# Second sorting pass carries projected rows, one stream for both directions of the first layer, and stage ends without the GpSimd drain

## The chip, the cores and the metric

The kernel runs on one core of a Trainium2 chip. The metric is the device time of one execution in microseconds (us). Its engines: PE (TensorE), DVE (VectorE), ACT (ScalarE), POOL (GpSimd) and SP (SyncE, which here only issues DMAs).

## The reference, cut to what matters

Four graph layers over N = 6250 nodes with 128 features and E = 106250 edges. Each is added to its input and normalized. The first is attention in both directions of every edge; layer 1 (two HGT sublayers), layer 2 (GCN) and layer 3 (GINE) go along `dst` alone.

```python
def _attention_aggregate(h_proj, sender, receiver, attn_vec, num_nodes):   # 4 heads of 32
    e = (h_proj[sender] . attn_vec[:, :HD]) + (h_proj[receiver] . attn_vec[:, HD:])
    e = leaky_relu(e, 0.2)
    alpha = exp(e - segment_max(e, receiver)[receiver])
    alpha = alpha / (segment_sum(alpha, receiver)[receiver] + 1e-8)
    return segment_sum(h_proj[sender] * alpha, receiver)
# layer 0: in = aggregate(src -> dst), out = aggregate(dst -> src),
#          y = layernorm(x @ W_self + in + out + bias); x = layernorm(x + y)
```

## The kernel before, in words

Nodes are padded to NB = 49 blocks of 128 (partition = node within the block). Edges lie in 128 partitions of EC = 832 columns. The program is 14 stages, one `Space` each; a stage allocates its buffers and semaphores, holds one block of five engine programs, and ends with engine drains, the clearing of its semaphores by GpSimd and a barrier of all engines (lines 59 to 70). Where the profile names L67 or L70, it means this end.

1. `load_inputs` and `count_keys` load the keys and count the edges of each node by `dst`.
2. `place_edges(k=1)` ("plc1") and `place_edges(k=0)` ("plc0") are two counting sorts, by `dst` and by `src`. Both read the input order `REC` (partner key, key, type, weight: RW = 4 words) and work in NCH = 104 chunks of CH = 8 columns. PE, DVE and ACT work out a slot for each of the 128 x 8 edges; POOL then issues 8 indirect DMAs (L843), each of which scatters 128 rows of 16 bytes into `slots`. `idx` has IB = 4 buffers, so DVE (`finish`, L637 to L645) may be at most four chunks ahead of what has landed. plc1 also counts by `src` (`count_more`) and zeroes DRAM. plc0 also projects x (`project`: PE L737 to L751, DVE `pack`), writes the row `h, scores` to `table0`, keeps x @ W_self in `g.HH` in SBUF, scatters the first-of-node scores of the `dst` side (L850), and builds the tables of the `dst` order (`table_part`).
3. `layer0_sweeps` ("l0") goes over the 832 columns twice, side 1 (`dst` order), then side 0 (`src` order): 104 chunks of CK = 16 columns. For each column POOL issues one indirect DMA (L951) that gathers 128 rows of W0 = 136 words from `table0` by the partner's number; `G` has GR = 4 chunk buffers. DVE's `logits` (L1082 to L1096) makes the scores and a running maximum; ACT (`powers`) makes the exponentials in PSUM (L1025 to L1029); DVE multiplies the rows (L1103) and scans them (L1108), the segment sum; ACT copies the result to `ROW` (L1037, L1038) and SP stores it to `sums`. DVE does these steps of one chunk before it begins the next. Beside it POOL also scatters 49 blocks of scores (L959) and fetches 49 blocks of sums of side 1 (L983), which DVE adds to `g.HH`. At the end of a side a short merge joins the partitions (L1119 to L1142, POOL L936 and L942).
4. `turn_layer` ("t0", "t1", "t2") fetches the last row of each node from `sums` by 49 indirect DMAs (L1682), normalizes groups of GT = 7 blocks on DVE and ACT (`close_part` in t0, seven parts that run seven blocks ahead), and projects block by block on PE; POOL scatters the queries of each block (L1689), from four buffers `qr`.
5. `attention_sweep` (L1245, rows of 256 words, twice), `plain_sweep` (L1501, twice), `turn_plain` and `close_all` do the other layers in the same way.

What sets the order: every engine runs its own program in order, written out by hand. POOL's queue carries all indirect DMAs; SP's carries the plain loads and stores; ACT's carries `low_rows` in the placings.

Of the kernel before, what the change touches and what calls it, by code (L numbers as in the profile page):

```python
# [5 lines left out]
P = 128  # L6
# [24 lines left out]
NCK = EC // CK  # L31
GR = 4
# [7 lines left out]
RW = 4  # L40
PART = 32
W0 = D + 2 * H
# [12 lines left out]
class Space:  # L55
# [22 lines left out]
    def sem(self, name):  # L78
        self.sems.append(self.nc.alloc_semaphore(f"{self.tag}_{name}"))
        return self.sems[-1]  # L80

    def block(self):
        return self.ctx.enter_context(self.nc.Block())
# [48 lines left out]
def load_inputs(nc, g, a):  # L132

    with Space(nc, "ld") as s:
# [34 lines left out]
        def _(pool):  # L169
# [17 lines left out]
            pool.iota(g.col[:, :], pattern=[[1, EC]], base=-EC, channel_multiplier=0,  # L187
                      allow_small_or_imprecise_dtypes=True).then_inc(made, 1)
# [8 lines left out]
        def _(v):  # L197
# [6 lines left out]
            v.wait_ge(made, 13)  # L204
# [16 lines left out]
            for k in (1, 0):  # L221
                v.tensor_copy(g.REC[:, :, k], keys[:, k, :])
# [3 lines left out]
                v.tensor_copy(g.LOW[:, k, :], lo[:, :])  # L226
                link(v.tensor_copy(g.DIG[:, k, 1, :], hi[:, :]))
            v.wait_ge(drawn_p, 2)
            v.tensor_copy(g.REC[:, :, 3], weights[:, :])
            link(v.tensor_copy(g.REC[:, :, 2], keys[:, 2, :]))  # L230
# [50 lines left out]
def count_keys(nc, g, a, k, tag):  # L281

    with Space(nc, tag) as s:
# [22 lines left out]
        def _(sp):  # L306
# [14 lines left out]
        def _(act):  # L321
            for c in range(3, NCH, 4):
                if c >= OB:
                    act.wait_ge(counted, c - OB + 1)
                for x in range(CH):
                    o = act.activation(column(olo[:, c % OB, :, :, :], x), g.iota_b[:, :], ACT.Square, scale=-1.0,
                                       bias=g.LOW[:, k, c * CH + x:c * CH + x + 1])
# [29 lines left out]
        def _(pe):  # L357
            pe.wait_ge(zeroed, 1)
            pe.matmul(pc[:, 0:NB], zero[:, :], zero[:, 0:NB], start=True, stop=False, skip_group_check=True)
            for c in range(NCH):  # L360
# [9 lines left out]
                if c in (8, 16):  # L370
                    n = c // 8 - 1
                    for q, (start, z) in enumerate(wide):
                        o = pe.transpose(px[0:z, n, q * P:(q + 1) * P], g.LOW[:, 1 - n, start:start + z], g.ident[:, :])
# [8 lines left out]
class Tables:  # L382


    def __init__(self, s):
# [6 lines left out]
        self.small = s.sb("tab_small", [P, 8])  # L392
        self.diag = s.sb("tab_diag", [P, 3, P])
        self.bc = s.sb("tab_bc", [P, 3, P])


TABLE_PARTS = 13
# [10 lines left out]
def table_part(v, link, g, b, k, pb, i):  # L408

    F, t, small, diag, bc = b.F, b.t, b.small, b.diag, b.bc  # L410
    own = b.rec[:, :, k]
    if i == 0:
        v.wait_ge(b.loaded, 32)
        v.tensor_copy(g.OTHI[:, k, :], b.rec[:, :, 1 - k])
    elif i == 1:
        if k == 1:
            v.scalar_tensor_tensor(out=g.KVI[:, :], in0=b.rec[:, :, 0], scalar=float(R), in1=b.rec[:, :, 2],
                                   op0=ALU.mult, op1=ALU.add)
            v.tensor_copy(g.WEIGHT[:, :], b.rec[:, :, 3])
    elif i == 2:  # L420
        v.tensor_tensor(F[:, 1:EC], own[:, 1:EC], own[:, 0:EC - 1], ALU.not_equal)
        link(v.tensor_tensor(F[:, 0:1], own[:, 0:1], b.prev[:, :], ALU.not_equal))
    elif i == 3:
        link(v.tensor_tensor(t[:, :], g.slot[:, :], F[:, :], ALU.mult))
        link(v.tensor_reduce(small[:, 0:1], t[:, :], AX.X, ALU.max))
    elif i == 4:
        link(v.tensor_tensor(t[:, 1:EC], g.col[:, 1:EC], F[:, 1:EC], ALU.mult))
        link(v.tensor_reduce(small[:, 1:2], t[:, 1:EC], AX.X, ALU.min))
    elif i == 5:
        v.tensor_scalar(diag[:, 0, :], g.ident[:, :], small[:, 0:1], None, ALU.mult)  # L430
        v.tensor_scalar(diag[:, 1, :], g.ident[:, :], own[:, 0:1], None, ALU.mult)
        v.tensor_scalar(diag[:, 2, :], g.ident[:, :], own[:, EC - 1:EC], None, ALU.mult).then_inc(b.ruled, 1)
    elif i == 6:
        v.wait_ge(b.spread, 1)
        v.tensor_copy(bc[:, :, :].rearrange("p a b -> p (a b)"), pb).then_inc(b.read, 1)
        v.wait_ge(b.read, 1)
        link(v.tensor_tensor(bc[:, 0, :], bc[:, 0, :], g.after[:, :], ALU.mult))
        link(v.tensor_reduce(small[:, 2:3], bc[:, 0, :], AX.X, ALU.max))
    elif i == 7:
        link(v.tensor_scalar(small[:, 2:3], small[:, 2:3], -1.0, g.head[:, 0:1], ALU.add, ALU.subtract))  # L440
        link(v.tensor_scalar(small[:, 3:4], F[:, 0:1], -1.0, 1.0, ALU.mult, ALU.add))
        link(v.tensor_tensor(small[:, 2:3], small[:, 2:3], small[:, 3:4], ALU.mult))
    elif i == 8:
        v.tensor_scalar(g.SEGI[:, k, :], small[:, 2:3], g.head[:, 0:1], None, ALU.add)
        v.tensor_copy(g.HEADI[:, k, :], g.head[:, :])
        link(v.tensor_scalar(small[:, 4:5], small[:, 1:2], float(EC - 1), g.head[:, 0:1], ALU.add, ALU.add))
        v.tensor_copy(g.FIRSTI[:, k, :], small[:, 4:5])
    elif i == 9:
        link(v.tensor_scalar(small[:, 5:6], small[:, 4:5], g.idle[:, 0:1], None, ALU.subtract))
        link(v.tensor_tensor(small[:, 5:6], small[:, 5:6], small[:, 3:4], ALU.mult))  # L450
        link(v.tensor_scalar(g.BACKI[:, k, :], small[:, 5:6], g.idle[:, 0:1], None, ALU.add))
    elif i == 10:
        link(v.tensor_scalar(bc[:, 1, :], bc[:, 1, :], own[:, EC - 1:EC], None, ALU.is_equal))
        link(v.tensor_tensor(g.MM[:, k, :], bc[:, 1, :], g.before[:, :], ALU.mult))
        link(v.tensor_scalar(bc[:, 2, :], bc[:, 2, :], own[:, 0:1], None, ALU.is_equal))
    elif i == 11:
# [2167 lines left out]
```

## Time and profile before

| what | us |
|---|---|
| three runs, median (lowest to highest) | 9965.67 (9952.68 to 9969.04) |
| the profiled execution, its own time | 9951.04 |
| its span, first to last instruction | 9949.3 |
| POOL busy | 6849.4 (69%) |
| DVE busy | 5464.7 (55%) |
| ACT busy | 3065.5 (31%) |
| PE busy | 2007.9 (20%) |
| DMA moved | 1161.90 MB, 117 GB/s |

Busy time does not count the time in which an engine's sequencer issues or waits. A row of a group of instructions has its count, its busy time, the mean of one in ns, and the idle time of the engine before them with what ended it; "issue" is time without a wait that the profile shows.

### The profile page before, as it was taken

Reading aid. Unit: us, or ns where it says so; the run is one execution under the profiler, and the core shown is the slowest. Engines: PE = TensorE matmul, PEld = TensorE weight load, DVE = VectorE, ACT = ScalarE, POOL = GpSimd, SP = SyncE. Lnnn points to the kernel's source line nnn. Section 1 sums busy time; section 2 is a strip of 40 time slices with the busy share of each in tenths; the row PEclk is TensorE's granted clock in tenths of the full one; section 3 lists DMA queues with packets and bytes.
Section 4 is the critical chain, followed back from the end, with each engine's and each line's share of the span. In section 5 each row is a group of like instructions: output and inputs, shape, how many; then the busy total and the mean of one; then the engine's idle time right before and its main releaser. Section 6 shows DMA issues by size and latency. Waiting matters only on the chain. (4 is left out here: it accounts for less than half of the span.)

```text
span 9949.3 us, 59877 instructions
## 1 busy us (share of the span) xinstructions
PE 2007.9 (20%) x16169; PEld 1858.3 (19%) x16169; DVE 5464.7 (55%) x9481; ACT 3065.5 (31%) x3237; POOL 6849.4 (69%) x7186
## 2 busy tenths in 40 slices
PE   5555465550000000002500007000032000200002
PEld 5555455550000000002500007000021000100002
DVE  7555454443545554556688884788874222432225
ACT  6333233331223332232355543454531000110002
POOL 3777677777777777775477763677745777577773
PEclk5555555555555555556855558555555555555556
DMA  5411111112333333334466654566642333233331
GB/s 163 147 28 29 33 35 34 33 29 64 99 99 115 110 110 107 104 113 138 166 217 211 213 192 168 192 214 213 212 140 77 105 103 108 82 96 104 105 107 58
DMA packets 490844, 1161.90 MB, mean 117 GB/s; under 512 B 184121, under 2 KB 279692, under 8 KB 432396
## 3 DMA queue, kind: packets, MB, share of 16 engines
q0 software_dynamic: 255936, 474.70, 17.8%
q1 hardware_dynamic: 204620, 628.82, 17.3%
q10 hardware_dynamic: 29952, 54.54, 2.0%
q8 instruction: 133, 2.18, 0.1%
q14 instruction: 203, 1.66, 0.1%
HBM read 669.61 MB, written 487.92 MB: 116 GB/s over the span
## 5 line engine op out<-in xcount | busy, mean ns | idle before, releaser
L843 POOL DMA_INDIRECT slots<-REC,plc_idx x1664 | 1597.8, 960 | 551.2 <-issue 505.6
L951 POOL DMA_INDIRECT l_G<-table,OTHI x1664 | 1585.8, 953 | 513.4 <-issue 505.6
L1245 POOL DMA_INDIRECT l_swp_G<-table,KVI x1664 | 1573.4, 946 | 529.2 <-issue 506.3
L1501 POOL DMA_INDIRECT l2s_G<-table,OTHI x832 | 785.0, 943 | 389.7 <-issue 253.3
L1501 POOL DMA_INDIRECT l3s_G<-table,OTHI x832 | 786.4, 945 | 301.6 <-issue 253.3
L714 PEld LDWEIGHTS plc_pr<-plc_seen,plc_otf 128*128 128x128 f32 x3328 | 846.6, 324 | 20.5 <-issue 11.8
L714 PE MATMUL plc_pr<-plc_seen,plc_otf 128*128 128x49 f32 x3328 | 847.7, 409 | 10.9 <-DVE plc_seen L628 10.9
L1348 DVE SCALAR_TENSOR_TENSOR l_swp_QS<-l_swp_QS,KEEP,l_swp_QX 128x128 f32<-128x128 f32 x1664 | 589.1, 354 | 45.6 <-DMA l_swp_QX<-queries 8.3
L645 DVE TENSOR_SCALAR plc_idx<-plc_pos 128x8 uint32<-128x8 f32 x208 | 36.4, 175 | 946.0 <-DMA slots<-REC,plc_idx 945.3
L1103 DVE TENSOR_TENSOR l_X<-l_G,l_AW 128x2048 f32<-128x2048 f32 x104 | 397.3, 3821 | 217.7 <-ACT l_X L1029 210.8
L1108 DVE TENSOR_TENSOR_SCAN l_X<-l_AW,l_X 128x2244 f32<-128x2244 f32 x104 | 502.5, 4832 | 3.6
L1407 DVE TENSOR_TENSOR_SCAN l_swp_X<-l_swp_AW,l_swp_X 128x2244 f32<-128x2244 f32 x104 | 501.5, 4822 | 0.1
L1082 DVE TENSOR_TENSOR l_LB<-l_RE,l_G 128x64 f32<-128x64 f32 x104 | 29.6, 284 | 793.7 <-DMA l_G<-table,OTHI 793.5
L1457 PE MATMUL l_swp_AW<-l_swp_ET,ones 128*128 128x512 f32 x4 | 4.2, 1142 | 2169.4 <-DVE l_swp_ET L1437 2169.4
L716 PEld LDWEIGHTS plc_pr<-plc_ohi,plc_bm 128*128 128x128 bf16 x1664 | 440.6, 265 | 0.0
L1296 ACT ACTIVATE l_swp_VT<-l_swp_G 128x2048 f32<-128x2048 f32 x104 | 385.9, 3711 | 73.7 <-DMA l_swp_G<-table,KVI 66.5
L1313 ACT ACTIVATE l_swp_ROW<-l_swp_X 128x2112 f32<-128x2112 f32 x104 | 407.6, 3919 | 0.0
L1038 ACT ACTIVATE l_ROW<-l_X 128x2112 f32<-128x2112 f32 x104 | 407.4, 3917 | 0.0
L1457 PEld LDWEIGHTS l_swp_AW<-l_swp_ET,ones 128*128 128x128 f32 x4 | 1.0, 312 | 2169.8 <-DVE l_swp_ET L1437 2169.8
L1578 DVE SCALAR_TENSOR_TENSOR l2s_S<-l2s_ROW,KEEP,l2s_G 128x128 f32<-128x128 f32 x52 | 18.7, 360 | 704.1 <-DMA l2s_G<-table,OTHI 704.1
L1578 DVE SCALAR_TENSOR_TENSOR l3s_S<-l3s_ROW,KEEP,l3s_G 128x128 f32<-128x128 f32 x52 | 18.7, 360 | 701.6 <-DMA l3s_G<-table,OTHI 701.6
L1186 PE MATMUL l_pr<-l_ET,ones 128*128 128x512 f32 x4 | 4.1, 1126 | 1958.8 <-DVE l_ET L1122 1958.8
(488 smaller groups left out, 9261.4 us busy)
## 6 DMA issues: line engine op xcount, KB each, us to landing
sums<-l_ROW SPq DMA_DIRECT2D x104, 1088.0 KB, 4.2
sums<-l_swp_ROW SPq DMA_DIRECT2D x104, 1088.0 KB, 5.2
l_swp_QX<-queries SPq DMA_DIRECT2D x104, 1024.0 KB, 8.0
queries<-plc_zrow SPq DMA_DIRECT2D x33, 1664.0 KB
sums<-l3s_ROW SPq DMA_DIRECT2D x52, 1032.0 KB, 4.3
plc_low<-low_rows ACTq DMA_DIRECT2D x208, 256.0 KB
sums<-l2s_ROW SPq DMA_DIRECT2D x52, 1024.0 KB, 4.4
table<-t_row SPq DMA_DIRECT2D x98, 512.0 KB, 2.9
```

The source lines that it names most:

```text
L714: pe.matmul(pr[:, b, j * NB:(j + 1) * NB], otf[:, c % FB, j, :], seen[:, b, :, j], start=True, stop=False)
L716: last = pe.matmul(pr[:, b, j * NB:(j + 1) * NB], bm[:, b, j, :], column(ohi[:, c % HB, :, :, :], j), start=False, stop=True)
L843: pool.indirect_dma_start(out=slots, out_offset=bass.IndirectOffsetOnAxis(ap=idx[:, c % IB, j:j + 1], axis=0), in_=g.REC[:, c * CH + j, :] ...
L951: pool.indirect_dma_start(out=G[:, c % GR, j, :], out_offset=None, in_=table, in_offset=bass.IndirectOffsetOnAxis(ap=g.OTHI[:, side(c), x: ...
L1038: act.activation(ROW[:, c % 2, :, 0:D + H], X[:, c % 2, :, :, 1:CK + 1].rearrange("p h d c -> p c (h d)"), ACT.Copy).then_inc(rowed, 1)
L1103: v.tensor_tensor(X[:, b, :, 0:HD, 1:CK + 1], G[:, c % GR, :, 0:D].rearrange("p c (h d) -> p h d c", h=H), W[:, :, :].rearrange("p h (o c) ...
L1108: v.tensor_tensor_scan(X[:, b, :, :, :].rearrange("p h d c -> p (h d c)"), AF[:, :, :, :].rearrange("p h d c -> p (h d c)"), X[:, b, :, :, ...
L1245: pool.indirect_dma_start(out=G[:, c % GR, j, :], out_offset=None, in_=table, in_offset=bass.IndirectOffsetOnAxis(ap=index[:, c * CK + j:c ...
L1313: act.activation(ROW[:, c % 2, :, 0:D + H], X[:, c % 2, :, :, 1:CK + 1].rearrange("p h d c -> p c (h d)"), ACT.Copy).then_inc(rowed, 1)
L1348: v.scalar_tensor_tensor(out=QS[:, j, :], in0=QS[:, j - 1 if j else QH - 1, :], scalar=g.KEEP[:, k, n:n + 1], in1=QX[:, c % QB, x, :], op0 ...
L1407: v.tensor_tensor_scan(X[:, b, :, :, :].rearrange("p h d c -> p (h d c)"), AF[:, :, :, :].rearrange("p h d c -> p (h d c)"), X[:, b, :, :, ...
L1501: pool.indirect_dma_start(out=G[:, c % GR, j, :], out_offset=None, in_=table, in_offset=bass.IndirectOffsetOnAxis(ap=g.OTHI[:, k, c * CK + ...
```

## The change

Records grow to RW = 5 words (low and high digit of `src`, `dst`, type, weight). plc1 stays the sort by `dst`, and now does the projection too: POOL issues 49 more scatters there (chunks 55 to 103), which put the row of each node (4 + 4 scores and h: WQ = 136 words) at the first slot of its segment in `queries`; x @ W_self goes to DRAM. Zeroing is spread over the blocks.

plc0 now reads the edges in `dst` order (the result of plc1), turns the digits of `src` itself, and DVE expands the rows: `expand` makes, for every column, "the row before, if in the same segment, plus what lies in `queries`". The scatter carries 132 words (score and h) instead of 4, into `arrived`. POOL issues the 49 scatters of `marks` first.

`layer0_sweeps` takes a chunk of side 0 and of side 1 in turn: side 0 comes from `arrived` by a plain load of SP (3 buffers `A`), side 1 by the gather of POOL. DVE does `logits` of the next chunk before `weigh` and `add_up` of this one. Both merges stand at the end. t0 fetches `sums[1]` as well and loads x @ W_self; its query scatters are issued between the fetches.

Stages end by `Block(no_gpsimd_drain=True)`, a clear of the semaphores by SP, and a barrier of semaphores alone; semaphores that a DMA of POOL raises (`landing`) are taken from the other end of the pool and are not cleared or used again.

```diff
-RW = 4
-W0 = D + 2 * H
+RW = 5
+W0 = D + H
+WQ = D + 2 * H
+AB = 3
+HEADS = 55
+AHEAD = 4
@@ Space
-            self.nc.clear_and_free_semaphores(self.sems)
-            self.nc.all_engine_barrier()
+            nc.sync.sem_clear(range(min(numbers), max(numbers) + 1))
+            nc.all_engine_barrier(sem_only=True)
...
-        return self.ctx.enter_context(self.nc.Block())
+        return self.ctx.enter_context(self.nc.Block(no_gpsimd_drain=True))
@@ place_edges, vector
+            def expand(c, j):
+                n = c * CH + j
...
+                if j == 0:
+                    v.wait_ge(qx_ok[c % XB], 16 * (c // XB + 1))
+                    if c >= IB:
+                        v.wait_ge(sent[c % IB], c // IB * (CH * 16))
+                v.wait_ge(rowed, n)
+                before = QS[:, c % IB, j - 1, :] if j else QS[:, (c - 1) % IB, CH - 1, :]
+                v.scalar_tensor_tensor(out=to, in0=before, scalar=g.KEEP[:, n:n + 1], in1=QX[:, c % XB, j, :],
+                                       op0=ALU.mult, op1=ALU.add).then_inc(rowed, 1)
@@ place_edges, gpsimd
+            if spread is not None:
+                for n in range(MARKED):
+                    start_mark(n)
+                pool.wait_ge(segd, 1)
...
+                for n in range(MARKED, NB):
+                    start_mark(n)
             for c in range(NCH):
                 pool.wait_ge(index_ok, c + 1)
+                if spread is not None:
+                    pool.wait_ge(rowed, (c + 1) * CH)
...
-                        in_=g.REC[:, c * CH + j, :], in_offset=None).then_inc(sent[c % IB], 16)
-                if project is not None and c % 2 == 1 and 0 <= (c - 5) // 2 < NB:
+                        in_=g.REC[:, c * CH + j, :] if spread is None else QS[:, c % IB, j, H:WQ],
+                        in_offset=None).then_inc(sent[c % IB], 16)
...
+                if project is not None and 0 <= c - HEADS < NB:
...
+                        out=heads_of, out_offset=bass.IndirectOffsetOnAxis(ap=g.STARTI[:, 1, n:n + 1], axis=0),
+                        in_=row[:, n, 0:WQ], in_offset=None).then_inc(put, 16)
@@ layer0_sweeps, gpsimd
-            for c in range(NC2):
-                if c >= GR:
-                    pool.wait_ge(used, c - GR + 1)
+            for p in range(NCK):
+                if p >= GR:
+                    pool.wait_ge(used, 2 * (p - GR) + 2)
...
+                        out=G[:, p % GR, j, :], out_offset=None, in_=table,
@@ layer0_sweeps, scalar
             def powers(c):
                 act.wait_ge(shifted, c + 1)
                 if c >= 1:
-                    act.wait_ge(carried, c)
-                act.activation(W[:, :, :], DW[:, c % 2, :, 1:CK + 1], ACT.Exp)
+                    act.wait_ge(used, c)
+                act.activation(W[:, :, :], DW[:, c % 2, :, 1:CK + 1], ACT.Exp).then_inc(weighed, 1)
...
+                if c >= 1:
+                    act.wait_ge(summed, c)
                 act.activation(AF[:, :, :, :],
...
             for c in range(NC2):
-                if c + 1 < NC2:
-                    flags(c + 1)
                 powers(c)
-                rows_of(c)
+                tops(c)
+                if c >= 1:
+                    rows_of(c - 1)
+                if c + 2 < NC2:
+                    flags(c + 2)
@@ layer0_sweeps, vector (table_part, reach, add_direction go)
-                link(v.tensor_scalar(T5[:, :, :], lg, 0.2, None, ALU.mult))
-                link(v.tensor_tensor(lg, lg, T5[:, :, :], ALU.max))
+                link(v.scalar_tensor_tensor(out=lg, in0=T5[:, :, :], scalar=0.2, in1=T5[:, :, :], op0=ALU.mult, op1=ALU.max))
...
-                v.tensor_copy(X[:, 1 - b, :, :, 0:1], X[:, b, :, :, CK:CK + 1]).then_inc(carried, 1)
...
+            logits(0)
             for c in range(NC2):
-                logits(c)
+                if c + 1 < NC2:
+                    logits(c + 1)
+                weigh(c)
                 add_up(c)
@@ turn_layer, gpsimd (t0)
+            if closes_l0:
+                for n in range(NB):
+                    fetch(n)
+                    fetch_in(n)
+                    if n >= AHEAD * GT - 1:
+                        put_query(n - AHEAD * GT + 1)
@@ turn_layer, vector, close_part
                 if j == 0:
+                    v.wait_ge(masks_ok[G], 48 if G < NG - 1 else 64)
                     link(v.tensor_tensor(hh, hh, flat(par[:, 0, :]), ALU.add))
-                    v.wait_ge(masks_ok[G], 32 if G < NG - 1 else 48)
                     link(v.tensor_tensor(x, x, flat(par[:, 2, :]), ALU.add))
-                    mean(G, 1e-8, sq)
+                    mean(G, 1e-8, sq, NV, RING, 2 * G + 1)
+                    link(v.tensor_tensor(hh, hh, sq, ALU.add))
                 elif j == 1:
+                    mean(G, 1e-8, sq, NI, AHEAD, 2 * G + 2)
                     link(v.tensor_tensor(hh, hh, sq, ALU.add))
@@ gnn_kernel
-                        place_edges(nc, g, 0, slots[0], "plc0", project=(a, table0, 1, slots[1], starts[1]))
-                    layer0_sweeps(nc, g, table0, starts, slots[0], (sums0, sums1), "l0")
+                place_edges(nc, g, 0, arrived, "plc0", spread=(slots, marks, queries))
+            layer0_sweeps(nc, g, table0, arrived, (sums0, sums1), "l0")
```

## Rows read from the trace of the kernel before

**Rows 1.** The page, part 1: busy time by engine, over the span.

```profile
PE 2007.9 (20%) x16169; PEld 1858.3 (19%) x16169; DVE 5464.7 (55%) x9481; ACT 3065.5 (31%) x3237; POOL 6849.4 (69%) x7186
```

**Rows 2.** Groups of instructions on POOL, whole span.

```profile
L843 POOL DMA_INDIRECT slots<-REC,plc_idx x1664 | 1597.8, 960 | 551.2 <-issue 505.6 <-DVE plc_idx L645 45.6
L951 POOL DMA_INDIRECT l_G<-table,OTHI x1664 | 1585.8, 953 | 513.4 <-issue 505.6 <-POOLq L70 6.5 <-DVE l_X L1103 1.2
...
L983 POOL DMA_INDIRECT l_tab_rec<-sums,LASTI x49 | 46.2, 943 | 14.9 <-issue 14.9
```

**Rows 3.** Timeline of POOL where plc1, plc0 and l0 begin or end: start, duration.

```profile
144.06 1.14 POOL L843 DMA_INDIRECT slots<-REC,plc_idx  x1 [14.42 <-DVE plc_idx L645]
...
1224.28 0.96 POOL L843 DMA_INDIRECT slots<-REC,plc_idx  x1 [29.95 <-DVE plc_idx L645]
...
2339.54 0.95 POOL L843 DMA_INDIRECT slots<-REC,plc_idx  x1 [0.30 <-issue]
...
2347.04 0.98 POOL L951 DMA_INDIRECT l_G<-table,OTHI  x1 [6.55 <-POOLq L70]
```

**Rows 4.** Groups of instructions in the stage l0 (2346 to 4610 us).

```profile
L1108 DVE TENSOR_TENSOR_SCAN l_X<-l_AW,l_X 128x2244 f32<-128x2244 f32 x104 | 502.5, 4832 | 3.6
L1038 ACT ACTIVATE l_ROW<-l_X 128x2112 f32<-128x2112 f32 x104 | 407.4, 3917 | 0.0
L1103 DVE TENSOR_TENSOR l_X<-l_G,l_AW 128x2048 f32<-128x2048 f32 x104 | 397.3, 3821 | 217.7 <-ACT l_X L1029 210.8 <-issue 5.1 <-DVE l_tab_F L422 0.9
L1026 ACT ACTIVATE l_AW<-l_Z 128x2244 f32<-128x2244 f32 x104 | 212.1, 2039 | 0.0
...
L1082 DVE TENSOR_TENSOR l_LB<-l_RE,l_G 128x64 f32<-128x64 f32 x104 | 29.6, 284 | 793.7 <-DMA l_G<-table,OTHI 793.5
```

**Rows 5.** Timeline of DVE in the last chunk of l0.

```profile
4575.25 0.28 DVE L1082 TENSOR_TENSOR l_LB<-l_RE,l_G 128x64 f32<-128x64 f32 x1 [4.44 <-DMA l_G<-table,OTHI]
...
4579.68 3.82 DVE L1103 TENSOR_TENSOR l_X<-l_G,l_AW 128x2048 f32<-128x2048 f32 x1 [2.44 <-ACT l_X L1029]
4583.54 4.83 DVE L1108 TENSOR_TENSOR_SCAN l_X<-l_AW,l_X 128x2244 f32<-128x2244 f32 x1
```

**Rows 6.** What ended DVE's idle time before L645 in plc0, with times, and a timeline row.

```profile
  DMA slots<-REC,plc_idx: 527.4, 97
...
5010.13 3.12 DVE L1348 SCALAR_TENSOR_TENSOR l_swp_QS<-l_swp_QS,KEEP,l_swp_QX 128x128 f32<-128x128 f32 x8
```

**Rows 7.** Timeline of t0: one issue of POOL and the DVE instruction beside it.

```profile
4674.48 1.77 POOL L1682 DMA_INDIRECT t_NV<-sums,LASTI  x1 [0.30 <-issue]
...
4674.34 1.09 DVE L1866 TENSOR_TENSOR X<-X,t_st 128x896 f32<-128x896 f32 x1
```

**Rows 8.** GpSimd's drain at the ends of six stages: ns, and when it began.

```profile
L67 POOLq DRAIN  x1: 5280/5280/5280, 1195.7 to 1195.7; - x1
...
L67 POOLq DRAIN  x1: 3479/3479/3479, 2341.9 to 2341.9; - x1
...
L67 POOLq DRAIN  x1: 8057/8057/8057, 4609.5 to 4609.5; - x1
...
L67 POOLq DRAIN  x1: 8216/8216/8216, 4884.0 to 4884.0; - x1
...
L67 POOLq DRAIN  x1: 5443/5443/5443, 5976.6 to 5976.6; - x1
...
L67 POOLq DRAIN  x1: 4132/4132/4132, 8598.9 to 8598.9; - x1
```

**Rows 9.** Stage t0: first mean of DVE, two scatters of POOL, busy times from 4720 to 4760.

```profile
4634.57 0.20 DVE L1829 TENSOR_SCALAR t_rec<-t_NV 128x28 f32<-128x28 f32 x1
...
4719.62 1.69 POOL L1689 DMA_INDIRECT queries<-t_qr,STARTI  x1 [4.07 <-ACT t_qr L2012]
...
4749.50 1.69 POOL L1689 DMA_INDIRECT queries<-t_qr,STARTI  x1 [4.07 <-ACT t_qr L2012]
...
4720.00:4760.00 40.00, 38.55 (x435) 35.63 (x434) 33.62 (x59) 17.35 (x42) 11.58 (x10) 1.00 0.46 169
```

More of the change, by code:

```diff
@@ L31 @@
 NCK = EC // CK
+WIDE = [(q * P, min(P, EC - q * P)) for q in range(-(-EC // P))]
 GR = 4
@@ L405, in load_slots @@
         sp.dma_start(b.prev[:, :], slots[0:P * EC, :].rearrange("(p c) w -> p c w", p=P)[:, 0, k:k + 1]).then_inc(b.loaded, 16)
[L408 to L456, printed above, removed]
-        link(v.tensor_tensor(bc[:, 2, :], bc[:, 2, :], g.after[:, :], ALU.mult))
-        link(v.tensor_scalar(g.PEN[:, k, :], bc[:, 2, :], -1.0, BIG, ALU.add, ALU.mult))
-        link(v.memset(F[:, 0:1], 1.0))
-    elif i == 12:
-        v.tensor_scalar(g.KEEP[:, k, :], F[:, :], -1.0, 1.0, ALU.mult, ALU.add)
-        link(v.tensor_scalar(g.FNEG[:, k, :], F[:, :], -BIG, None, ALU.mult))
@@ L521, in place_edges @@
             ht = s.sb("ht", [P, 2, P])
-            row = s.sb("row", [P, 2, W0])
+            selves = s.sb("selves", [P, OW, D])
+            row = g.rows_x
+            p2 = s.ps("p2", [P, 512])
+            h_at = P + 2 * H
+            own_at = h_at + D + 2 * H
+        if spread is not None:
+            records, marks, expanded = spread
+            b_ = Tables(s)
+            lows = s.sb("lows", [P, len(WIDE), P], BF16)
+            digit_ok, turned, lows_ok, lows_out = s.sem("digit_ok"), s.sem("turned"), s.sem("lows_ok"), s.sem("lows_out")
+            qx_ok = [s.sem(f"qx_ok{b}") for b in range(XB)]
+            rowed, segd, emptied, lined = (s.sem(x) for x in ("rowed", "segd", "emptied", "lined"))
+            taken, put, marked = (s.landing(x) for x in ("taken", "put", "marked"))
+            QX = s.sb("QX", [P, XB, CH, WQ])
+            QS = s.sb("QS", [P, IB, CH, WQ])
+            first = s.sb("first", [P, WQ])
+            mark = s.sb("mark", [P, MW])
+            lines = b_.rec
@@ new lines, in _ @@
+            for c in range(-3, NCH + 1):
+                if project is not None and c % 2 == 0 and 0 <= c // 2 - 1 < NB:
+                    pack(c // 2 - 1)
+                n = c + 1
+                expand(n, 0)
+                if 0 <= n < NCH:
+                    keep_earlier(n)
+                expand(n, 1)
+                if 0 <= n < NCH:
+                    counted_so_far(n)
+                    expand(n, 2)
+                    count_up(n)
+                expand(n, 3)
+                if 0 <= c + 3 < NCH and not (spread is not None and c + 3 < 2):
+                    low_digits(c + 3)
+                    expand(n, 4)
+                    high_digits(c + 3)
+                else:
+                    expand(n, 4)
+                expand(n, 5)
@@ L1473, in plain_sweep @@
     with Space(nc, tag) as s:
-        gathered = [s.sem(f"gathered{r}") for r in range(GR)]
+        gathered = [s.landing(f"gathered{r}") for r in range(GR)]
         summed, used, rowed, chain, spread, merged = (
```

927 lines of the change are left out of this document (529 added, 398 removed).

## The prediction, made before the changed kernel was run

> **What bounds the kernel now.** I read the page's busy times first. No engine but POOL is above 55%, and POOL stands at 69% [rows 1]. The groups of POOL show that this is less slack than it looks: the 1664 scatters of the two placings take 0.960 us each and carry 505.6 us of "issue" idle, so one comes every (1597.8 + 505.6) / 1664 = 1.264 us; the 1664 gathers of l0 come every (1585.8 + 505.6) / 1664 = 1.257 us [rows 2]. Nothing but the next instruction fills that idle time. A scatter of 16-byte rows costs the same as a gather of 544-byte rows, so POOL's price is per instruction, not per byte. The other engines wait for it: in l0, 793.7 us of idle DVE ended with the landing of a gather [rows 4], and in plc0 DVE waited 97 times, 527.4 us in all, for a scatter to land [rows 6]. So the time of the placings and sweeps is the number of indirect DMAs times 1.26 us, plus the ends of the stages. The question is how many issues go, and which engine limits the stage that loses them.
>
> **l0, before.** It runs from 2347.04 [rows 3] to the drain at 4609.5 [rows 8], 2262 us. POOL issues 1664 + 49 + 49 and a few: 1.257 x 1766 = 2220, the rest is the first landing and the tail.
>
> **l0, after.** POOL keeps 832 gathers: 16 x 1.257 = 20.1 us for a pair of chunks (one of each side). DVE must do two chunks in that time. In the last chunk before, the eight small instructions of `logits` run from 4575.25 to 4579.68 - 2.44 = 4577.24, that is 1.99 us [rows 5]. One of them goes (a multiply and a maximum become one), about 0.27, so 1.72. The product is 3.82 and the scan 4.83 with 0.04 between each [rows 5], the group means say the same [rows 4]. The small copy after the scan goes to ACT. A chunk is 1.72 + 3.86 + 4.87 = 10.45, a pair 20.9: DVE now decides, by 0.8 us. ACT has 2.04 + 3.92 [rows 4] and about 1.2 of small ones, 7.2 per chunk, and its long exponential stands beside `logits` and the product of DVE, which give it 5.6 us, so it is hidden. If that cover were gone it would be exposed by its 2.04. Stage: 22 us until the first gathered chunk is there (16 x 1.257 and a landing), 104 x 10.45 = 1087 less the first `logits`, and a tail: before it was 4609.5 - 4588.4 = 21 us from the last scan [rows 5, 8]; with two merges in lockstep I take 26. Sum 1133. Term: 1133 - 2263 = **-1130**. Bounds: DVE can't do better than POOL, which would be 52 x 0.8 = 42 less; a DVE slower by 3% through the added traffic is 33 more.
>
> **plc1** gets 49 scatters more on POOL: 49 x 1.264 = +62. They lie behind chunk 55, when the rows are there and the zeroing long over, so nothing is added to their wait. The projection costs DVE half a `pack` per chunk; in plc0, where it stood, DVE had 527.4 / 97 = 5.4 us of waits per chunk [rows 6], in plc1 the count by `src` takes two compares of that, and cover remains. The lead-in was 14.42 us of idle POOL before 144.06 [rows 3]; the ACT copy of the type masks and the loads of x now stand ahead of it: +3, between 0 and +6. Term: **+65**.
>
> **plc0** issues 832 + 49 before and 832 + 49 + 2 after: +2.5. Its lead-in shortens: before, POOL stood 29.95 us ahead of 1224.28 [rows 3], 23 of them after the drain's end at 1195.7 + 5.28 = 1201.0 [rows 8]. Now POOL has 49 scatters of marks to issue (62 us) while the records load and the first chunk is worked out, so only a wait of 0 to 6 for the first take remains: -20. DVE gets eight expanding instructions per chunk. Back to back such a one is 3.12 / 8 = 0.39 us [rows 6], so 3.1 and a copy of 0.2, against 5.4 of waits, of which the projection frees another 0.4. DVE is at some 8 of 10.1 us: hidden. POOL's `rowed` wait asks for rows that DVE made one chunk earlier, so it adds nothing.
>
> The one new price is contention. An issue of POOL that began at 4674.48 took 1.77 us, where the mean of gathers is 0.95 [rows 2], and ended its extra 0.82 where DVE's product of two SBUF tensors ended (4674.34 + 1.09) [rows 7]; in l0, where the products read PSUM beside SBUF, the mean is 0.953 [rows 2]. `expand` reads `QS` and `QX`, both in SBUF. By the width (896 elements in 1.09 us) its 136 take about 0.16 us, so 8 x 0.16 / 10.1 = 13% of the issues wait 0.08 on average: 0.13 x 0.08 x 832 = 9 us. Were the whole 0.39 held, it is 31% x 0.19 x 832 = 49 us. I take 10, since the lock follows the data in the row; both ends are kept.
>
> The Trainium skill (SBUF — State Buffer, "Who interferes with whom") says that a DVE instruction with two SBUF inputs contends with a GpSimd instruction that reads SBUF, and that whoever came first keeps the shared pair for the whole instruction. It adds that descriptor generation was not seen to be held by such products; the row of this case shows that an indirect one is. Held for the whole instruction, it is the upper end above.
>
> Term of plc0: 2.5 - 20 + 10 = **-8**.
>
> **t0** gets 49 fetches, and DVE the second mean. Before, the first mean began at 4634.57 [rows 9], 17 us after the drain's end at 4617.6 [rows 8]. Now 14 fetches must land first, 14 x 1.257 and a landing, some 24 us, and the second mean follows with one addition: +11. Then the blocks run with PE busy 38.55 of 40 us, and one group of seven takes 4749.50 - 4719.62 = 29.9 us [rows 9]. DVE has 33.62 of 40, 25.1 per group; two 896-wide instructions of 1.09 [rows 7] and two short ones make 27.8. PE stays the bound, but the additions fall on two blocks where DVE is already late (the scatters at 4719.62 and 4749.50 came with the longest waits, 4.07). I take 1.2 of the 2.7 per group, +7. POOL issues three per block there, 3.8 us against 4.3. Term: **+18**, between 0 and 11 + 6 x 2.7 + 3 = +30.
>
> **The ends of the stages.** GpSimd's drain lasts 5.28 after plc1, 3.48 after plc0, 8.06 after l0, 8.22 after t0 and the same after t1, 5.44 after each attention sweep, 4.13 after each plain sweep [rows 8], where three of the six rows stand for two ends each. In these nine nothing else was late: 5.28 + 3.48 + 8.06 + 2 x 8.22 + 2 x 5.44 + 2 x 4.13 = 52.4 us. After t2 and t3 the drain ended before the work did. What is late next is the barrier and SP's clear, as before. Term: **-51**, between -40 and -56.
>
> The counting stage loses one transposition and a copy of ACT: -1. The attention sweeps load 136 words for 128 from `queries` under POOL's cover: 0, at most +5.
>
> **Sum.** -1130 + 65 - 8 + 18 - 51 - 1 = -1107. The profiled execution took 9951.04: 8844. The median of the three runs stands 14.6 above it; I forecast **8850** for the median, between the two. Differences under 0.2% (18 us) can't be told from none here.
>
> **Rivals.** *l0 stays a chain.* If `logits` and the product did not cover ACT's exponentials, a chunk would last as long as the last one before, 4583.54 + 4.83 - 4575.25 = 13.1 us [rows 5]: 104 x 2.7 = +280, 9130. For it: one PSUM buffer holds the factors. Against: its release is the scan, and 5.6 us of DVE work lie after that. Chance 0.07. *plc0 becomes bound by DVE.* The added 3.3 us against 5.8 of waits would have to grow by stalls between PE and DVE to 11 us a chunk: +94, 8945. Chance 0.10. *The port holds POOL for the whole expanding instruction*: +39, 8890. The hold is seen [rows 7]; its length for a short instruction isn't shown. Chance 0.08. This is the way it goes by the rule of the Trainium skill (SBUF — State Buffer, "Who interferes with whom"). *Slower than before.* The place is plc0, where a scatter now writes 128 rows of 528 bytes to random places. It decides from the point at which the writes land more slowly than 1.264 + 1107 / 832 = 2.6 us each; at 2.8 us the kernel would be at 8850 + 832 x 1.53 = 10120. Against it: gathers of 544-byte rows ran at 1.257 [rows 2]. Chance 0.02. *The change doesn't do what it says*: the waits for landings behind a semaphore take the place of the drains, +51, 8900. Against: the drains begin after those waits. Chance 0.03. That leaves 0.69 for the forecast, and 0.01 for an end within 0.2% of before.
>
> **How the numbers follow.** The forecast's own bounds are 8844 - 42 - 18 - 5 = about 8780 and 8850 + 33 + 12 + 5 = 8900. To leave out no more than 2 in 10, the range reaches over the port and over DVE in plc0: 8780 to 8960. Faster 0.97, same 0.01, slower 0.02.
>
> **What would show it.** Right: 832 gathers in l0, DVE over 95% busy there with the scan and the product at the same means, and a pair every 21 us; scatters in plc0 every 1.264 us, some of them stretched; POOLq's drain gone from the ends; plc1 longer by 65. Wrong: idle DVE before the product with ACT as releaser in l0; POOL waiting for `plc_idx` or the expanded rows in plc0; scatters whose mean is above 1.05 us; long waits for `A` or for stored sums, which would mean that DMA decides.

## The result and the profile after

The median is **8815.40 us** (8814.85 to 8820.33) against 9967.35 (9952.68 to 9969.20) for the kernel before in the same series: ratio 0.885, 95% interval 0.883 to 0.886. The forecast was 8850, the range 8780 to 8960. The profiled execution has a span of 8813.4, 1135.9 shorter than the one before; the sum of the prediction had 1107. The forecast of 8850 lay 6 us above that sum, between the profile before and the median before; here the profiled execution (8815.13) lies at the median.

The page of the kernel after: span, busy times, and groups (busy time, mean in ns, then the idle time before them with its releaser).

```profile
span 8813.4 us, 60467 instructions
...
PE 2052.3 (23%) x16367; PEld 1898.9 (22%) x16367; DVE 5593.5 (63%) x10159; ACT 3091.3 (35%) x3341; POOL 6086.1 (69%) x6351
...
L1065 POOL DMA_INDIRECT arrived<-plc_QS,plc_idx x832 | 812.3, 976 | 253.5 <-issue 244.3
L1065 POOL DMA_INDIRECT slots<-REC,plc_idx x832 | 798.5, 960 | 273.1 <-issue 251.7
L1150 POOL DMA_INDIRECT l_G<-table,OTHI x832 | 790.1, 950 | 256.1 <-issue 253.0
...
L1287 DVE TENSOR_TENSOR_SCAN l_X<-l_AW,l_X 128x2244 f32<-128x2244 f32 x104 | 502.5, 4831 | 3.6
...
L735 DVE SCALAR_TENSOR_TENSOR plc_QS<-plc_QS,KEEP,plc_QX 128x136 f32<-128x136 f32 x831 | 289.0, 348 | 323.3 <-DMA arrived<-plc_QS,plc_idx 200.1
```

POOL's share is still 69%: it lost 763 us of work, and the span lost 1136. The price of one indirect DMA is nearly as it was [rows 2]: 528-byte rows scatter at (812.3 + 253.5) / 832 = 1.281 us, with 8.8 us of waits and the holding described below in it, 20-byte rows at 1.288 with the stage's start in it, gathers at 1.257. What fell is their number: from 7166 to 6332 in the program, and from 1770 to 836 in l0.

Where one stage ends and the next begins on POOL (start, duration, instruction, and in brackets the idle time before it):

```profile
148.01 1.13 POOL L1065 DMA_INDIRECT slots<-REC,plc_idx  x1 [19.93 <-DVE plc_idx L697]
...
1260.71 0.96 POOL L1080 DMA_INDIRECT queries<-shared,STARTI  x1 [0.30 <-issue]
1264.37 0.96 POOL L1047 DMA_INDIRECT marks<-NS,STARTI  x1 [2.70 <-POOLq L83]
...
2398.44 0.95 POOL L1065 DMA_INDIRECT arrived<-plc_QS,plc_idx  x1 [0.30 <-issue]
2402.22 0.98 POOL L1150 DMA_INDIRECT l_G<-table,OTHI  x1 [2.83 <-POOLq L83]
...
3444.67 0.94 POOL L1150 DMA_INDIRECT l_G<-table,OTHI  x1 [0.30 <-issue]
3481.44 0.94 POOL L1156 DMA_INDIRECT l_FR<-sums,FIRSTI  x1 [35.82 <-DMA sums<-l_ROW]
...
3499.46 0.97 POOL L1161 DMA_INDIRECT sums<-l_FR,BACKI  x1 [0.63 <-issue]
3503.16 0.97 POOL L1845 DMA_INDIRECT t_NV<-sums,LASTI  x1 [2.72 <-POOLq L83]
...
3779.45 0.98 POOL L1886 DMA_INDIRECT queries<-t_first,HEADI  x1 [2.45 <-DMA t_first<-queries,SEGI]
3783.26 0.97 POOL L1405 DMA_INDIRECT l_swp_G<-table,KVI  x1 [2.84 <-POOLq L83]
```

An end costs 2.7 to 2.8 us now (2.2 at the last of the nine), where it cost 6.55 ahead of l0 [rows 3] and 11.10 ahead of t0. Read this way for both kernels, a stage being the time from POOL's first instruction in it to its last, the whole difference is found:

| part | before | after | difference | forecast |
|---|---|---|---|---|
| counting, to the first instruction of plc1 | 126.8 | 126.2 | -0.6 | -1 |
| plc1: lead-in | 17.3 | 21.8 | +4.6 | +3 |
| plc1: scatters | 1050.3 | 1113.7 | +63.4 | +62 |
| end of plc1 and plc0 | 1146.2 | 1137.7 | -8.5 | -13 (-8, and 5 of the ends) |
| l0 | 2261.0 | 1098.2 | -1162.8 | -1130 |
| t0 | 263.5 | 277.3 | +13.8 | +18 |
| eight other ends | 70.8 | 21.5 | -49.3 | -46 |
| all the rest (sweeps, t1, t2, last stages) | | | +3.4 | 0 |
| sum | 9949.3 | 8813.4 | -1136 | -1107 |

Of the 29 us by which the sum is off, l0 holds 33. Its chunks on DVE, one whole from scan to scan:

```profile
2898.65 4.83 DVE L1287 TENSOR_TENSOR_SCAN l_X<-l_AW,l_X 128x2244 f32<-128x2244 f32 x1
2903.40 0.15 DVE L1257 COPY l_LB<-l_M 128x4 f32<-128x4 f32 x1
2903.45 0.26 DVE L1258 TENSOR_TENSOR l_T<-shared,l_A 128x64 f32<-128x64 f32 x1
2903.74 0.23 DVE L1260 SCALAR_TENSOR_TENSOR l_LB<-l_T 128x64 f32<-128x64 f32 x1
2904.01 0.29 DVE L1264 TENSOR_TENSOR_SCAN l_M<-l_FL,l_LB 128x68 f32<-128x68 f32 x1
2904.34 0.22 DVE L1268 TENSOR_TENSOR l_DW<-l_LB,l_M 128x64 f32<-128x64 f32 x1
2904.48 0.21 DVE L1269 TENSOR_TENSOR l_Z<-l_M 128x64 f32<-128x64 f32 x1
2904.73 0.23 DVE L1270 TENSOR_TENSOR l_Z<-l_Z,l_FL 128x64 f32<-128x64 f32 x1
2904.87 3.83 DVE L1278 TENSOR_TENSOR l_X<-l_G,l_WP 128x2048 f32<-128x2048 f32 x1
2908.74 4.83 DVE L1287 TENSOR_TENSOR_SCAN l_X<-l_AW,l_X 128x2244 f32<-128x2244 f32 x1
```

A chunk is 2908.74 - 2898.65 = 10.09 us: 4.75 from the scan's start to the copy, 1.47 for `logits`, 3.87 for the product. The prediction had 4.87, 1.72 and 3.86. The copy begins 0.08 before the scan's end. So does every instruction here that does not wait for the one ahead of it: L1258, L1269 and L1278 begin 0.08 to 0.10 before the end of L1257, L1268 and L1270. One that waits begins 0.03 to 0.05 after that end. The waits of DVE in l0 (total, times, longest):

```profile
DVE l_LB L1257 <- DMA l_G<-table,OTHI: 20.3, 2, 15.6
DVE l_LB L1257 <- DMA l_A<-arrived: 4.2, 1, 4.2
```

They all lie at the start. So in the steady part DVE never waits: it is busy for 1017.2 of the 1040 us from 2430 to 3470, and two chunks take 20.2 us. POOL issues 16 gathers in 16 x (3444.67 - 2402.22) / 831 = 20.07 us and never waits either, but its four buffers let it run ahead, and after its last gather it waits 35.82 us for DVE's last rows to be stored (the row of L1156 above). The two engines are level to within 1%.

### The profile page after: what moved, and what is told of

Its sections match the earlier page's. It is cut to its first block and busy times, and to the rows that moved or that the text cites. A ratio compares the mean times of both kernels' runs of the same rounds, so it can differ in the third digit from the quotient of the medians.

```text
span 8813.4 us, 60467 instructions
## 1 busy us (share of the span) xinstructions
PE 2052.3 (23%) x16367; PEld 1898.9 (22%) x16367; DVE 5593.5 (63%) x10159; ACT 3091.3 (35%) x3341; POOL 6086.1 (69%) x6351
## 5 line engine op out<-in xcount | busy, mean ns | idle before, releaser
L1065 POOL DMA_INDIRECT arrived<-plc_QS,plc_idx x832 | 812.3, 976 | 253.5 <-issue 244.3
L1065 POOL DMA_INDIRECT slots<-REC,plc_idx x832 | 798.5, 960 | 273.1 <-issue 251.7
L1150 POOL DMA_INDIRECT l_G<-table,OTHI x832 | 790.1, 950 | 256.1 <-issue 253.0
L735 DVE SCALAR_TENSOR_TENSOR plc_QS<-plc_QS,KEEP,plc_QX 128x136 f32<-128x136 f32 x831 | 289.0, 348 | 323.3 <-DMA arrived<-plc_QS,plc_idx 200.1
L1018 ACT ACTIVATE plc_otb<-plc_otf 128x1024 bf16<-128x1024 f32 x208 | 219.9, 1057 | 699.9 <-PE plc_pe_q L893 698.0
L1698 ACT ACTIVATE l2s_ROW<-l2s_S 128x1920 f32<-128x1920 f32 x52 | 92.1, 1771 | 964.6 <-DVE l2s_ROW L1738 964.6
L1514 DVE TENSOR_TENSOR l_swp_PROD<-l_swp_G,l_swp_QS 128x1024 f32<-128x1024 f32 x208 | 254.0, 1221 | 261.3 <-DMA l_swp_G<-table,KVI 260.6
```

Source lines behind the costliest of these rows:

```text
L735: v.scalar_tensor_tensor(out=to, in0=before, scalar=g.KEEP[:, n:n + 1], in1=QX[:, c % XB, j, :], op0=ALU.mult, op1=ALU.add).then_inc(rowed, 1)
L1065: pool.indirect_dma_start(out=slots, out_offset=bass.IndirectOffsetOnAxis(ap=idx[:, c % IB, j:j + 1], axis=0), in_=g.REC[:, c * CH + j, :] ...
L1150: pool.indirect_dma_start(out=G[:, p % GR, j, :], out_offset=None, in_=table, in_offset=bass.IndirectOffsetOnAxis(ap=g.OTHI[:, x:x + 1], a ...
```

## The experiments

Three questions: what carries l0's rate, what the ends are worth, and what two inputs in SBUF cost POOL. Ratios are to the kernel before, run beside each.

### The stage ends

The first is the kernel before with the exit of a stage, `block` and `landing` of the new one (as in the change's diff), the semaphores that POOL's DMAs raise taken by `landing`. The second is the kernel after with this line back:

```diff
-        return self.ctx.enter_context(self.nc.Block(no_gpsimd_drain=True))
+        return self.ctx.enter_context(self.nc.Block())
```

> The kernel before with the new stage ends alone (no drain of GpSimd, semaphores cleared by SyncE, barrier of semaphores, landing semaphores kept out of the clearing). My theory, by the gaps in POOL's row between the stages of the two kernels: 54.6 us go (5.3 after plc1, 3.7, 8.4, 8.6, 5.8, 8.6, 5.8, 4.3, 4.2 at the others), so about 9897 in a profile and a ratio to before near 0.9945. Rival: the drain only moved, and a wait for landings or for the semaphores takes its place: a ratio within 0.001 of 1.

Measured: 9893.24 us against 9951.46, ratio 0.994 (0.993 to 0.995), -58.2. That is the 54.6 us that were expected and 3.6 more. The nine gaps of POOL between the stages lose 55.6 us; the long stages keep their times to 1.2 us each. The rival is out.

> The changed kernel with the drain of GpSimd back at the end of each block, all else kept (clearing by SyncE, barrier of semaphores). My theory: the drain itself was the price of the ends, and 45 to 56 us come back: a span of 8858 to 8870, with the first instruction of POOL in a stage again 6 to 11 us behind the last of the stage before. Rival: the clearing by GpSimd and the barrier with drains of the other engines carried part of it, and less than 35 us come back.

Measured: 8856.37 us, ratio 0.890 (0.889 to 0.891), span 8852.7, which is 5 us below the expected range of spans. In this series the placings and the attention sweeps lasted 1 to 3 us less each than in the profile after, so the difference of spans, 39, understates it. (The clock is not the reason: `expand_one_input`, on the same chip at the clock of the profile after, 0.53, has these shorter sweeps too.) Against the next two kernels, which ran on the same chip, the time outside l0 is the measure: 8852.7 - 1098.3 = 7754.4 here, 9076.2 - 1368.0 = 7708.2 in `weights_in_sbuf`: **46 us**. Summed over the nine gaps it is 49.9. The gap ahead of t0 with the drain, and the drain itself (ns, and when it began):

```profile
3503.98 0.97 POOL L1161 DMA_INDIRECT sums<-l_FR,BACKI  x1 [0.63 <-issue]
3512.00 0.98 POOL L1845 DMA_INDIRECT t_NV<-sums,LASTI  x1 [7.05 <-POOLq L83]
```

```profile
L78 POOLq DRAIN  x1: 4288/4288/4288, 3506.4 to 3506.4; - x1
```

It is 7.05, not the 11.10 of before, because the drain is shorter: 4.29 us where it was 8.06 [rows 8]. From the drain's end to POOL's next instruction it is 1.28 us here and 1.56 before, so the clearing by GpSimd and the barrier with drains made 0.3 us of this end, and 0.1 to 0.4 of the others that can be compared. The nine drains last 49.5 us together in `drain_back` and 52.4 before: so of the 58 us of `ends_only` the drains are 52. Behind the sweeps, which the change leaves alone, a drain keeps its length (5.44 and 5.43, 4.13 and 4.13); behind l0 it fell from 8.06 to 4.29 and behind plc0 it rose from 3.48 to 5.28. What sets its length is not shown.

### Two inputs in SBUF beside an indirect DMA

`expand_one_input` leaves out an addition, as its expectation says:

```diff
-                v.scalar_tensor_tensor(out=to, in0=before, scalar=g.KEEP[:, n:n + 1], in1=QX[:, c % XB, j, :],
-                                       op0=ALU.mult, op1=ALU.add).then_inc(rowed, 1)
+                v.tensor_scalar(to, before, g.KEEP[:, n:n + 1], 0.0, ALU.mult, ALU.add).then_inc(rowed, 1)
```

> The changed kernel with expand as a multiplication of one SBUF input (the addition of the row of queries is left out, so attention rows are not the reference's). My theory: the scatters of plc0 are held only while an instruction of VectorE with two SBUF inputs runs, so the 79 held issues beside expand (8.25 us of extra in the trace of the changed kernel) go, the mean of these scatters falls from 976 to about 966 ns, and the stage gets 8 us shorter; the 10 us that the table's long instructions cost stay. Rival: the extra comes from the traffic of the scattered rows or of the SBUF reads as such; then the mean stays at 976.

Measured: 8800.89 us, ratio 0.884 (0.883 to 0.886); plc0 from its first to its last issue 1127.7 us, beside 1132.3 and 1131.9 in the two other kernels of this chip: 4 to 5 us, half of what was expected. The group of these scatters:

```profile
L1064 POOL DMA_INDIRECT arrived<-plc_QS,plc_idx x832 | 804.9, 967 | 253.7 <-issue 238.7 <-DVE plc_idx L697 14.6 <-DMA arrived<-plc_QS,plc_idx 0.3
```

The mean fell from 974 to 967 ns. In the profile after, 236 scatters began while an expanding instruction ran; 91 of them took over 20 ns more than usual, 9.0 us together. With one input it is 46 of 149, 2.5 us together. The rest of the gain went into waits for `idx` (14.6 us against 8.8). In both kernels nearly all the lengthened scatters ended 0.83 us after the end of the expansion that they met. So such a scatter is held until the instruction ends, and the form with one input holds too: "held only while an instruction of VectorE with two SBUF inputs runs" was wrong in its "only". (The factors `KEEP`, one for each partition, still come from SBUF in this edit, so it is no clean test of one input. But in the profile after, a cast of 0.94 us (`DIG`, L815), whose one input lies in SBUF, held a scatter of `marks` as well: it took 1.26 us and ended 0.84 after the cast.)

`weights_in_sbuf` moves 64 words of each partition:

```diff
-        W = WP[:, 0:H * CK].rearrange("p (h c) -> p h c", h=H)
+        W = s.sb("WS", [P, H, CK])
```

> The changed kernel with the 64 factors of l0's product in SBUF instead of PSUM: the product then reads two SBUF inputs for 3.85 us. Theory A: an indirect DMA's issue is held until such an instruction ends, whatever its length. Of each chunk 3.85 us are closed to POOL, and 8 issues need 8 x 1.254 beside them, less about half an issue of overlap: 13.4 us a chunk instead of 10.1, +300 to +360 us, span 9110 to 9180, with gathers of up to 4.8 us. Theory B: an issue is held for a short part alone (0.1 us, as beside the expansions): the gathers gain 0.1 us each in 38% of the cases, +30 us at most, span 8815 to 8845.

Measured: 9079.47 us, ratio 0.912 (0.911 to 0.914), span 9076.2. l0 lasts 1368.0 us, 270 more. The gathers and one of them beside the product:

```profile
L1150 POOL DMA_INDIRECT l_G<-table,OTHI x832 | 1072.9, 1290 | 256.1 <-issue 253.2
```

```profile
2805.38 0.94 POOL L1150 DMA_INDIRECT l_G<-table,OTHI  x1 [0.30 <-issue]
...
2806.14 3.79 DVE L1278 TENSOR_TENSOR l_X<-l_A,l_WS 128x2048 f32<-128x2048 f32 x1
2806.63 4.08 POOL L1150 DMA_INDIRECT l_G<-table,OTHI  x1 [0.30 <-issue]
...
2809.97 4.83 DVE L1287 TENSOR_TENSOR_SCAN l_X<-l_AW,l_X 128x2244 f32<-128x2244 f32 x1
...
2811.01 0.94 POOL L1150 DMA_INDIRECT l_G<-table,OTHI  x1 [0.30 <-issue]
```

The gather issued at 2806.63 took 4.08 us instead of 0.94 and ended 0.78 us after the product. All 102 gathers of l0 that began while the product ran were held so, by 2.8 us on average, and none of the 730 others. Theory A holds; its size was too large, as a gather under way when the product starts still finishes, and a chunk loses 2.6 us and not 3.3. Of the 308 gathers that began during the same product with its factors in PSUM, in the profile after, none was held; nor was any of the 206 in the attention sweeps that began during the 1.22 us product of `G` in SBUF and `QS` in PSUM. The 0.26 us addition L1258 of l0, both of whose inputs lie in SBUF, did hold 34 of 40. So for these instructions with two inputs it isn't the width that decides; where the second input lies does. The Trainium skill (SBUF — State Buffer, "Who interferes with whom") says that an instruction with two SBUF inputs contends with a GpSimd instruction that reads SBUF, and calls the shared pair of ports an exclusive lock; this agrees. That `tensor_tensor` was not seen stalling a DMA, which it also reports, doesn't hold for these DMAs.

### What carries l0's rate

Four kernels change the order on DVE (the lookahead) and what the product waits for, or halve the product:

```diff
@@ no_lookahead
-            logits(0)
             for c in range(NC2):
-                if c + 1 < NC2:
-                    logits(c + 1)
+                logits(c)
                 weigh(c)
@@ lookahead_all_powers (no_lookahead_all_powers has both)
-                v.wait_ge(weighed, c + 1)
+                v.wait_ge(powered, c + 1)
@@ half_product
-                v.tensor_tensor(X[:, b, :, 0:HD, 1:CK + 1],
+                v.tensor_tensor(X[:, b, :, 0:HD // 2, 1:CK + 1],
...
-            link(v.memset(X[:, :, :, :, 0:1], 0.0))
+            link(v.memset(X[:, :, :, :, :], 0.0))
```

> The changed kernel, l0 with logits, weigh and add_up of a chunk in a row on VectorE (no logits ahead). My theory: what matters is that the product waits for the small exponential alone (0.2 us on ACT) while the long one (2.06) runs beside the product; a chunk gets 0.4 to 0.5 longer for the hand-over to ACT: +40 to +55 us, span 8855 to 8870. Rival (the chain of my prediction): without logits ahead a chunk is a chain of 13.1 us, +310, span near 9120.

> As no_lookahead, and the product waits for all three exponentials of its chunk, as it did before the change. Both theories: the chain of before, logits 1.5, hand-over and exponentials 2.9, product 3.9, scan 4.8, that is 12.9 to 13.2 us a chunk, +290 to +320 us, span 9100 to 9135.

> The changed kernel with logits ahead, but the product waits for all three exponentials. My theory: the long exponential writes the one PSUM buffer that the scan of the chunk before frees, so it starts at that scan's end; logits of the next chunk cover 1.5 of its 2.1 us, and 0.7 to 0.9 us a chunk are exposed: +70 to +95 us, span 8885 to 8910. Rival: logits ahead hides ACT wholly, +0.

> The changed kernel with l0's product over half of the columns of h (the other half of the rows is left at zero and out of the result; one longer clearing of X at the start). Question: which engine sets l0's 20.2 us a pair. My theory: VectorE (98% busy) and POOL (16 x 1.254 = 20.06) are level, so taking 1.9 us from each chunk of VectorE gains only 50 x 0.17 = 9 us and a tail shorter by some 8: l0 at about 1080 instead of 1098, span 8790 to 8800, VectorE idle for 3 to 4 us a pair with the landing of G as its releaser. Rival: VectorE alone decides and POOL has room: 104 x 1.9 = -198, span near 8615.

These four ran on a chip on which the kernel before itself took 11448.77 us (median of nine), 15% more than elsewhere. Measured there: 10313.68 (ratio 0.901), 10412.43 (0.910), 10315.92 (0.901), 10307.91 (0.900). Their spans can't be held against 8813.4. In the page of `no_lookahead` PE and POOL wait where they did not:

```profile
L1065 POOL DMA_INDIRECT slots<-REC,plc_idx x832 | 796.7, 958 | 576.8 <-DVE plc_idx L697 322.9
L904 PE MATMUL plc_pr<-plc_seen,plc_otf 128*128 128x49 f32 x3328 | 862.6, 392 | 353.0 <-issue 350.5
```

Instructions last no longer than elsewhere (958 ns, 392 ns; 960 and 414 in the profile after), but 350 us pass ahead of one kind of matmul with no releaser but "issue" (12 us in the profile after, all of it a wait for DVE), and less ahead of others. Why this chip is so is open. Even there the change keeps a ratio of 0.90. The same kernels were run again, where before took 9951:

> The kernel of half_product again, since the first four of this kind ran where the kernel before itself took 11449 us, and instruction streams stopped for 1 us now and then. Here the clearing of X is 4 us longer, nothing else is new. My theory: VectorE and POOL are level in l0, so l0 lasts 1080 to 1088 us instead of 1098 and VectorE gets idle before the reading of G; span 8785 to 8800. Rival: VectorE alone decides and POOL has room: l0 near 900.

> The kernel of no_lookahead again, for the same reason. By the chunks of the first run (12.6 us with a stop of 1.0 in them, and a product that starts 0.4 later) my theory is: 0.4 to 0.5 us a chunk, l0 1140 to 1155 us instead of 1098, span 8845 to 8865. Rival (the chain of my prediction): 13.1 us a chunk, l0 near 1410.

> The kernel of no_lookahead_all_powers again, beside a kernel before at its usual time. In the first run a chunk without a stop lasted 12.6 us on VectorE, with 2.41 of waiting for the long exponential ahead of the product. My theory: 104 x 12.6 = 1310 and lead-in and tail of some 45: l0 1350 to 1360 us instead of 1098, span 9060 to 9080. The rival by my prediction's chain: 13.1 a chunk, l0 1400 to 1410, span near 9120.

> The kernel of lookahead_all_powers again. In its first run VectorE waited 2 x 15 us for the long exponential in all, not 0.8 a chunk. Theory now: logits of the next chunk (1.5) plus the hand-over cover all but 0.2 to 0.3 of it: l0 1115 to 1130 us, span 8825 to 8845. Rival (my first): 0.7 to 0.9 us a chunk exposed, span 8885 to 8910.

| kernel | median us | ratio, 95% interval | l0 us | chunk on DVE us |
|---|---|---|---|---|
| after (profile) | 8815.40 | 0.885 (0.883 to 0.886) | 1098.2 | 10.09 |
| half_product_2 | 8786.18 | 0.883 (0.882 to 0.884) | 1078.7 | 8.24, and a wait for G every second one |
| no_lookahead_2 | 8834.70 | 0.888 (0.886 to 0.889) | 1122.9 | 10.48 |
| lookahead_all_powers_2 | 8880.94 | 0.893 (0.891 to 0.894) | 1173.4 | 10.85 |
| no_lookahead_all_powers_2 | 9049.56 | 0.909 (0.908 to 0.911) | 1342.7 | 12.62 |

DVE's main wait in l0, in the order of the table from its second row:

```profile
DVE l_LB L1257 <- DMA l_G<-table,OTHI: 187.0, 49, 15.4
```

```profile
DVE l_X L1278 <- ACT l_WP L1200: 30.5, 104, 0.3
```

```profile
DVE l_X L1278 <- ACT l_AW L1206: 67.0, 102, 2.1
```

```profile
DVE l_X L1278 <- ACT l_AW L1206: 248.3, 103, 2.4
```

*Half the product.* It falls from 3.84 to 1.99 us, so DVE has 104 x 1.85 = 192 us less to do, and l0 gets 19.5 shorter: DVE's waits for the gathers rise from 20.3 to 187.0 us, which takes nearly all the rest back. That shows POOL right behind DVE. A faster product buys next to nothing here; the rival is out, and the theory's 1080 to 1088 was 1 us too high.

*Lookahead and early release, each with and without the other.* The chain of 12.6 us a chunk comes back (1342.7) only when both are undone. The early release of the product (it waits for ACT's exponential of 0.2 us, not for the one of 2.06) is worth 1342.7 - 1122.9 = 220 us alone, and 75 beside the lookahead. The lookahead is worth 169 alone and 25 beside the early release. Either would have done most of it, since both hide the same 2 us of ACT. What is left of the wait is 0.29 us a chunk in `no_lookahead_2` and 0.65 in `lookahead_all_powers_2`.

`no_lookahead_2` came out 17 us better than the low end of its expectation: it costs 0.39 a chunk, 40 in all, but its first chunk no longer waits for the first gather, and DVE's waits for `G` are 6.4 us instead of 20.3. For `no_lookahead_all_powers_2` the chunk of 12.6 was as expected, but l0 came out 7 us under its range and the span 13 under its own: lead-in and tail took 32 us and not 45. For `lookahead_all_powers` the first expectation (0.7 to 0.9 a chunk) was nearly right; the revised one was drawn from the run on the other chip, where DVE waited more for other things and this wait was hidden, and was wrong.

## Why the prediction was right, and where it was off

*What bounds the kernel.* "The number of indirect DMAs times 1.26 us, plus the ends of the stages" holds: in plc1, plc0 and the other sweeps POOL has hardly a wait besides "issue" and the ends.

*l0*: -1163 against -1130, the largest miss, within 9 us of its own lower bound; the mechanism held. The step that failed is "a chunk is 1.72 + 3.86 + 4.87 = 10.45". It measured 10.09 or 10.10. `logits` was taken as the old 1.99 less one instruction of 0.27; but the copy moved to the front, where nothing waits for it, so the next instruction follows 0.05 behind its start, and it begins before the scan has ended; the product, too, begins 0.09 before the end of the last small instruction. 104 x 0.35 = 36 us. The tail measured 3500.43 - (3474.26 + 4.83) = 21.3 and not 26; the lead-in was 22.9 as taken, but there was a second wait of 4.7 for the second set of gathers, which the sum did not have. "DVE now decides, by 0.8 us" a pair became 0.1 us: right in kind, and shown by the half product.

*"ACT's long exponential is hidden. If that cover were gone it would be exposed by its 2.04."* With all cover gone the product waits 2.4 (its hand-over included); with `logits` alone as cover 0.65. The rival of the chain was priced at 13.1 a chunk and measures 12.62. Its chance of 0.07 was fair: of the two steps that the change takes against it, one alone leaves 25 or 75 us of it.

*plc1*: +68 against +65. 49 scatters at 1.264 are 62, as said; the lead-in took 4.6 instead of 3, inside its bounds.

*plc0*: the end of plc1 and plc0 gave 8.5 where 13.3 were forecast. The lead-in vanished, better than said: no wait is left behind the marks. Holding cost more: 18.6 us over the stage by the trace, where before it was 4.3, and not 10. The expansions took 9.0 of it. That this is the lower bound of 9 is luck: it took them for 0.16 us long, by the width, and they last 0.35. What had been left out are the long two-input instructions that build the stage's tables (four scans cost 3.99 us, four others 4.2). The rival "the port holds POOL for the whole expanding instruction" was right as a mechanism: the held scatters end 0.83 us after the expansion, and `weights_in_sbuf` shows the same for gathers. It was wrong in price, 49 for 9. The share of issues that meet an expansion was nearly right (31%; 236 of 832 are 28%), but a scatter loses only what is left of the expansion after its own first 0.13 us, and 91 of the 236 lost anything.

*plc0 bound by DVE* did not come: DVE still waited 200.1 us for scatters to land. The expansions keep it busy for 289.0 / 104 = 2.8 us a chunk, inside the 3.3 that were taken.

*t0*: +13.8 against +18. From the first fetch to the first scatter of queries it grew from 65.1 to 75.5 us, 10.4 where 11 were forecast; from there to the last such scatter from 189.7 to 193.0, 3.3 where 7 were. Its gathers and scatters were held some 21 us in all, beside some 12 before.

*The ends*: the eight others lost 49.3, and the one of plc1 5.9 by `ends_only`: 55 against 51. The drains' own durations are 52.4 of it, as the prediction had summed them; it took 51, and what came on top is the shorter way through clearing and barrier, some 0.3 us an end.

*The sweeps*: they lost 0.8 to 1.8 us each. In the other runs of the changed kernel beside a before of 9951 they take 1079.7 to 1081.2, where before had 1081.1 and 1079.9, so this does not come from the wider rows of `queries`.

## What to carry to other kernels

Where one engine issues all indirect DMAs at a fixed price, count them first; bytes in the row were free here from 20 to 544. Before speeding up the engine that a stage seems to wait for, look how far behind it the next one is: half a product less gave 19 us of 192. And keep one input of every long VectorE instruction in PSUM while GpSimd issues: 64 words of each partition in the wrong memory cost 270 us.

## What the runs showed of the hardware

- An indirect DMA's issue that begins during a VectorE instruction with both inputs in SBUF lasts until 0.8 us after that instruction's end (4.08 us beside a product of 3.79; 102 of 102 gathers in `weights_in_sbuf`), for gathers and scatters alike. With one input in PSUM none of 308 was held. A form with one input, in SBUF, held 46 of 149 scatters in `expand_one_input`.
- The drain of GpSimd at a stage end lasts 3.5 to 8.8 us behind indirect DMAs, 52.4 us over nine ends before and 49.5 in `drain_back`. Clearing semaphores by GpSimd and a barrier with drains took 0.1 to 0.4 us more at an end than the clear by SyncE and the barrier of semaphores.
- A VectorE instruction that doesn't wait for the one ahead starts 0.08 to 0.10 us before its end, behind a copy of 0.15 us as behind a scan of 4.83; one that waits for it starts 0.03 to 0.05 us after its end.
- One chip ran the kernel before in 11449 us where others took 9951. In the changed kernel's profile there, instructions last no longer (958 ns a scatter) and 350 us of gaps stand ahead of one kind of matmul.
